# A perceiver block on one core: scores, values and side work of four attention steps in another order

## The chip, the cores and the metric

The kernel runs on one core of one Trainium2 chip. The time is the device time of one execution in microseconds: 961.16 us, the median of 3 runs (959.98 to 962.28). The profile shows another execution, which took 961.61 us.

## The reference, cut to what matters

```python
x = x + xattn(layernorm(x), ctx, ctx)   # x: 4 x 256 x 256, ctx: 4 x 4096 x 256, 16 heads of 16
x = x + attn(layernorm(x))              # linear attention by exponential features
x = x + ffn(layernorm(x))               # silu-gated, hidden size 768

# xattn:
Q, K, V = q @ Wq.T + bq, ctx @ Wk.T + bk, ctx @ Wv.T + bv
out = softmax(Q K^T / 4) V              # per head, 256 queries x 4096 keys
return out @ Wh.T + bh
# attn: per head causal, with features exp(clip(proj(x / |x|) * sqrt(2s) - s)) of q and k
```

All data are float32; some products run on high and low parts in a reduced float format.

## The kernel before, in words

There are four batches. The context of a batch, 4096 keys, is worked through in 8 chunks of 512 keys (`NCH`). A chunk has 16 steps (`STEPS`): a step takes 128 keys and 4 heads. Four steps are a quad, so a chunk has 4 quads, a batch 32 quads (128 steps), the kernel 128 quads.

A step has three parts. `fast_scores` (line 768, matmuls at L745) lets TensorE write the scores of 128 keys x 4 heads x 256 queries into one of two PSUM tiles ps_s, so it waits until the exponential of the step two before has read the tile. ScalarE takes the exponential into one of five buffers probs (L1011, `AHEAD`). `fast_values` (matmuls at L733) multiplies probs with the values and adds up in ps_o; it waits for its own exponential.

Between them lies side work, hung to step numbers: the slots. `fast_slot` of a step issues, on TensorE (line 782) and in the same order on VectorE (line 1347):
- projections of later chunks, into the one bank ps_p: values of the next chunk in steps 3 and 5 of a chunk (`VALUE_SLOTS`, L585), keys of the chunk after that in steps 9 and 13 (`KEY_SLOTS`, L552). VectorE copies them out (L1065; L1048 and L1050). In step 15 it also splits a piece of context into high and low parts (L1034, L1036);
- the stages of the tail of the batch before (everything behind the cross attention) and of the head of the next one (layernorm, queries, a bound for the scores), at the steps of the tables `AT` and `HEAD_AT` (counted within a batch). Nearly all of them write the one bank ps_a, which VectorE must have emptied before the next stage may write it. Stages named below: o, oT0, oT1 (1, 3, 4), ln1T, qk0, qk1 (24 to 26), qkT0, qkT1 (35, 36), feat0 to feat7 (feature products, L671, which VectorE clamps at L1249 and ScalarE exponentiates at L989), A0 to A15 (L677, L678), pv0 to pv3 (L682), y2T (91), wout (92, L615), ln2T (96, L607), gu0 to gu5 (gate products, L690, read by ScalarE, then by VectorE at L1259), down (121); of the head ln0T (102), q (106), max0 to max3 (112, 114, 116, 118).

The place of a slot is its step modulo 4. In the order before, a quad is: scores of places 0 and 1, their slots, scores of places 2 and 3, their slots, and then four value steps, which lag by two steps (`LAG`). In the first quad of a chunk the two value steps still due come between the halves and two come at the end. The first batch has no tail, the last no head.

ScalarE runs the exponentials in order of steps and takes the features and gates in between, where `ACT_BEHIND` says: behind the odd step of a pair.

Of the kernel before, what the change touches and what calls it, by code (L numbers as in the profile page):

```python
# [13 lines left out]
B, S, D = 4, 256, 256  # L14
# [13 lines left out]
QUAD = 2 * 2  # L28
# [19 lines left out]
LAG = 2  # L48
# [29 lines left out]
AT = {"o": 1, "oT0": 3, "oT1": 4, "yT": 19, "wh": 20, "ln1T": 24, "qk0": 25, "ss0": 25, "qk1": 26, "ss1": 26, "v": 28,  # L78
      "norm0": 34, "qkT0": 35, "norm1": 36, "qkT1": 36, "feat0": 37, **dict(zip(LINEAR, LINEAR_AT)),
      "o2T0": 88, "o2T1": 89, "y2T": 91, "wout": 92, "ln2T": 96, "gu0": 99, "gate0": 100, "gu1": 101, "gate1": 104,  # L80
      "gu2": 105, "gate2": 108, "gu3": 109, "gate3": 113, "gu4": 115, "gate4": 116, "gu5": 117, "gate5": 120,
      "down": 121}
# [5 lines left out]
FEATS = [f"feat{p}" for p in range(H // 2)]  # L88
GATES = [f"gu{k}" for k in range(HB)]

ACT_BEHIND = {**{n: 1 - AT[n] % 2 for n in FEATS}, **{n: 1 - AT[n] % 2 for n in GATES}}

NEEDS = {"maxT": "max3", "oT0": "o", "oT1": "o", "qk1": "ln1T", "v": "ln1T", "qkT0": "norm0", "qkT1": "norm1",
         **{n: "qkT1" for n in FEATS}, **{f"A{h}": "qkT1" for h in range(H)},
# [89 lines left out]
BS = NCH * STEPS  # L184
# [11 lines left out]
def perceiver(nc, x, ctxT, wqT, bq, wkT, bk, wvT, bv, whT, bh, wqkv, bqkv, wout, bout,  # L196
              omega, nodes, weights, wgT, wuT, wdT, out):
    ctx = ExitStack()
    with ctx:
# [120 lines left out]
        def tail_of(b):  # L320
            return (b + 2, b, True)

        def stages_at(b, step):

            return [(n, tail_of(of) if n in TAIL else head_of(of)) for of, n in stages_of(b, step)]
# [215 lines left out]
        def _(pe):  # L541
# [22 lines left out]
            def project_keys(q, j):  # L564

                pe.wait_ge(fast["ctx_split"], q + 1)
                if j:
                    pe.wait_ge(fast["k_out"], q * 2 + 1)
                elif q:
                    pe.wait_ge(fast["v_ready"], q * PAIRS)  # L570
                for part in range(CI):
                    project(fast, ("k", j, part), q, q % 2)

            def project_values(q, pair):

                if pair:
                    pe.wait_ge(fast["v_ready"], q * PAIRS + pair)
                else:
                    pe.wait_ge(fast["k_out"], q * 2 + 2)
                hi, lo = ctx_hi[q % 2], ctx_lo[q % 2]  # L580
                for t in range(2):
                    rows = slice((2 * pair + t) * P, (2 * pair + t + 1) * P)
                    for k in range(CI):
                        for n, (a, w) in enumerate(((hi, wv[0]), (lo, wv[0]), (hi, wv[1]))):
                            last = mm(ps_p[:, t * D:(t + 1) * D], a[:, k, rows], w[:, k, :],  # L585
                                      start=(t == 0 and k == 0 and n == 0), stop=(k == CI - 1 and n == 2),
                                      skip_group_check=True)
                last.then_inc(fast["v_proj"], 1)
# [123 lines left out]
            def products(c, names, clock, alone=False):  # L712
                for name in names:
                    if alone and c is fast:
                        warm(ps_o, WARM.get(name, 0))
                    if alone and name[:4] == "gate" and name != "gate0":

                        down_part(c, int(name[4:]) - 1, ps_a, clock)
                    if name not in VECTOR_ONLY:
                        stage(c, name, clock, alone)  # L720

            def value_product(c, n, s, par, starts, stops, vtile):

                i, g = s // G, s % G
                pe.wait_ge(c["exp_done"], n + (3 if c is general else 1))
                if c is general and g == 0:
                    pe.wait_ge(c["v_ready"], vtile + 2)
                elif c is fast and s % (STEPS // PAIRS) == 0:
                    pe.wait_ge(c["v_ready"], vtile // 2 + 1)
                prob = probs[s % NPROB if c is general else n % AHEAD]  # L730
                for j in range(GH):

                    last = mm(ps_o[32 * j:32 * j + DH + 1, g * S:(g + 1) * S],  # L733
                              values[par][:, i, head_of_step(g, j), :], prob[:, j * S:(j + 1) * S],
                              start=bool(starts and i == 0 and g % 2 == 0),
                              stop=bool(stops and i == TT - 1), skip_group_check=True)
                last.then_inc(c["pv_done"], 1)
# [30 lines left out]
            def fast_scores(b, q, s):  # L768

                n = q * STEPS + s  # L770
                if n >= LAG:
                    pe.wait_ge(fast["exp_done"], n - LAG + 1)
                score(fast, s, q % 2, qstacks[b % 2])

            def fast_values(n):

                b, q, s = n // BS, n // STEPS, n % STEPS
                if b and n % BS == 0:
                    pe.wait_ge(fast["operand"], fast.at("operand", tail_of(b - 1), "o"))
                value_product(fast, n, s, q % 2, q % NCH == 0, q % NCH == NCH - 1, q * TT + s // G)  # L780

            def fast_slot(b, p, s):

                q = b * NCH + p
                if s in VALUE_SLOTS and q + 1 < B * NCH:
                    project_values(q + 1, VALUE_SLOTS[s])
                if s in KEY_SLOTS and q + 2 < B * NCH:
                    project_keys(q + 2, KEY_SLOTS[s])
                for name, clock in stages_at(b, p * STEPS + s):
                    products(fast, [name], clock)  # L790
# [21 lines left out]
            for b in range(B):  # L812
                for p in range(NCH):
                    q = b * NCH + p
                    if p == 0:
                        pe.wait_ge(fast["q_stacked"], (b + 1) * Q_STACKED)
                        pe.wait_ge(fast["q_shift"], (b + 1) * 16)
                    if p == 0 and b == 1:
                        pe.wait_ge(late_in, 16 * 15)
                        pe.wait_ge(w_ready, 1)  # L820
                    if q < 2:
                        pe.wait_ge(hot_in, 16 * (q + 1))
                    pe.wait_ge(fast["k_stacked"][p % 2], (q // 2 + 1) * STACKED)
                    for s in range(0, STEPS, QUAD):
                        n = q * STEPS + s
                        for t in (0, 1):
                            fast_scores(b, q, s + t)
                        for t in (0, 1):
                            fast_slot(b, p, s + t)
                        if s == 0 and n:  # L830
                            for t in (0, 1):
                                fast_values(n - LAG + t)
                        for t in (2, 3):
                            fast_scores(b, q, s + t)
                        for t in (2, 3):
                            fast_slot(b, p, s + t)
                        for t in range(LAG if s == 0 else 0, QUAD):
                            fast_values(n - LAG + t)
            for t in range(LAG):
                fast_values(B * BS + t - LAG)  # L840
            products(fast, TAIL[:NORMALISED], tail_of(B - 1), True)

            pe.wait_ge(judged, 1)
# [133 lines left out]
        def _(act):  # L977
# [6 lines left out]
            def stage(c, name, clock, alone=False):  # L984
                if name in FEATS:
                    p = FEATS.index(name)

                    act.wait_ge(c["operand"], c.at("operand", clock, name))
                    nc.scalar.activation(feat[:, p % 2, :, :], feat[:, p % 2, :, :], ACT.Exp, bias=node_neg[:, :]  # L989
                                         ).then_inc(c["acted"], 1)  # L990
                else:
                    k = GATES.index(name)
                    act.wait_ge(c["product"], c.at("product", clock, name))
                    bank = bank_of(c, name, clock, alone)
                    nc.scalar.activation(gate_e[:, k % 2, :], bank[:, 0:S], ACT.Tanh, scale=QUANT / 2)
                    nc.scalar.activation(up[:, k % 2, :], bank[:, S:2 * S], ACT.Copy).then_inc(c["acted"], 1)
# [10 lines left out]
            for n in range(B * BS):  # L1007
# [5 lines left out]
                for name in FEATS + GATES:  # L1013
                    if n >= BS and AT[name] + ACT_BEHIND[name] == n % BS:
                        stage(fast, name, tail_of(n // BS - 1))
# [437 lines left out]
```

## Time and profile before

| | |
|---|---|
| median of 3 runs | 961.16 us (959.98 to 962.28) |
| the profiled execution | 961.61 us, span 959.9 us |
| TensorE busy | 872.1 us, 91% |
| TensorE weight loads | 608.0 us, 63% |
| ScalarE busy | 536.0 us, 56% |
| VectorE busy | 443.8 us, 46% |
| mean granted TensorE clock | 0.99 |
| chain that ended last | TensorE 73%, VectorE 11%, issue 6%, ScalarE 5% |

The attention steps run from 42.8 to 858 us; ahead of them lies the setup, behind them the tail of the last batch alone. Matmuls are pipelined: their durations overlap, so the time that a group takes is best read from its start to the start of the next. A clock of 1.00 is 2.4 GHz, 0.50 is 1.2 GHz.

### The profile page before, as it was taken

The numbers are of one execution on the slowest core, as the hardware profiler recorded it, in microseconds if no ns is written. First come the engines' busy times: TensorE is split into PE (matmuls) and PEld (weight loads), VectorE is DVE, ScalarE is ACT, GpSimd is POOL, SyncE is SP. The second block draws the span as 40 slices with busy tenths as digits, with TensorE's granted clock in tenths as the row PEclk, the third lists the DMA queues.
The fourth block names the chain that finished last, engine by engine and source line by source line (L and its number), as shares of the span: only waits on it lengthen the run. The fifth ranks groups of instructions, "written<-read, shape, count | busy, mean of one in ns | idle before, by whom it ended". The sixth has DMA issues, their size and how long they took to land.

```text
span 959.9 us, 20721 instructions
## 1 busy us (share of the span) xinstructions
PE 872.1 (91%) x8803; PEld 608.0 (63%) x8803; DVE 443.8 (46%) x847; ACT 536.0 (56%) x594; POOL 68.3 (7%) x124
## 2 busy tenths in 40 slices
PE   6799999999999988999999998999999999978676
PEld 5566666666566666666666665676666666656565
DVE  5522334554744345544743445535554444224553
ACT  2177777676565655656566555657566566840111
POOL 1033000000010000000011000000000000000120
PEclk9899999999999999999999999999999999999899
DMA  5666553566232333436233332345333331201000
GB/s 164 239 216 227 206 181 139 188 219 188 78 147 85 111 114 130 152 107 210 72 144 121 111 133 100 126 139 175 123 131 113 132 111 45 67 24 23 1 1 13
DMA packets 58736, 120.08 MB, mean 125 GB/s; under 512 B 21520, under 2 KB 29712, under 8 KB 55120
## 3 DMA queue, kind: packets, MB, share of 16 engines
q1 hardware_dynamic: 56848, 114.31, 34.6%
q0 software_dynamic: 1792, 4.40, 1.5%
q8 instruction: 71, 1.16, 0.5%
q14 instruction: 25, 0.20, 0.1%
HBM read 78.84 MB, written 37.75 MB: 121 GB/s over the span
## 4 chain that ended last, share of the span: by engine, by line
PE 73%; DVE 11%; issue 6%; ACT 5%; DVEq 2%; DMA 1%; POOL 1%; SPq 0%; ACTq 0%; POOLq 0%
PE ps_o L733 20%; PE ps_s L745 14%; PE ps_p L552 10%; PE ps_p L585 10%; ACT probs L1011 5%; PE ps_a L677 3%; PE ps_a L703 2%; PE ps_a L615 2%; PE ps_a L671 2%; PE ps_a L690 2%; DVE kparts L1050 1%; DVE kparts L1048 1%; PE ps_a L678 1%; DVE feat L1249 1%; PE ps_a L631 1%
## 5 line engine op out<-in xcount | busy, mean ns | idle before, releaser
L1011 ACT ACTIVATE probs<-ps_s 128x1024 f32<-128x1024 f32 x512 | 495.5, 1025 | 263.8 <-PE ps_s L745 236.1
L733 PE MATMUL ps_o<-probs,values 128*17 128x256 f32 x4096 | 252.0, 381 | 0.0
L745 PE MATMUL ps_s<-qstack,kstack 64*128 64x256 f32 x2048 | 201.4, 309 | 19.3 <-ACT probs L1011 18.5
L745 PEld LDWEIGHTS ps_s<-qstack,kstack 64*128 64x128 f32 x2048 | 140.7, 185 | 121.1 <-ACT probs L1011 65.1
L733 PEld LDWEIGHTS ps_o<-probs,values 128*17 128x17 f32 x4096 | 105.2, 97 | 93.1 <-issue 7.3
L1048 DVE TENSOR_SCALAR kparts<-ps_p,b_heads 128x512 fp32r<-128x512 f32 x64 | 48.0, 750 | 114.1 <-PE ps_p L552 114.0
L1065 DVE TENSOR_TENSOR values<-ps_p,bv_pair 128x512 f32<-128x512 f32 x64 | 44.2, 691 | 88.5 <-PE ps_p L585 88.5
L989 ACT ACTIVATE feat<-feat,node_neg 128x512 f32<-128x512 f32 x32 | 23.1, 722 | 105.4 <-DVE feat L1249 105.4
L585 PE MATMUL ps_p<-wv_hi,ctx_hi 128*128 128x256 f32 x256 | 78.6, 307 | 1.6 <-DVE wv_lo L1036 1.6
L585 PE MATMUL ps_p<-wv_hi,ctx_lo 128*128 128x256 f32 x256 | 72.3, 283 | 0.0
L585 PE MATMUL ps_p<-wv_lo,ctx_hi 128*128 128x256 f32 x256 | 72.3, 282 | 0.0
L552 PE MATMUL ps_p<-ctx_hi,wk_hi 128*128 128x512 f32 x128 | 58.8, 459 | 4.0 <-DVE ctx_lo L1036 2.2
L1253 DVE TENSOR_TENSOR amat<-ps_a,causal 128x384 f32<-128x384 f32 x48 | 26.7, 556 | 77.2 <-PE ps_a L678 77.2
L948 POOL TENSOR_TENSOR kfeat<-feat,half_mask 128x256 f32<-128x256 f32 x64 | 37.8, 612 | 313.7 <-ACT feat L989 313.7
L585 PEld LDWEIGHTS ps_p<-wv_hi,ctx_hi 128*128 128x128 f32 x256 | 48.4, 189 | 5.9 <-DVE wv_lo L1036 1.8
L552 PE MATMUL ps_p<-ctx_lo,wk_hi 128*128 128x512 f32 x128 | 51.9, 406 | 0.0
L552 PE MATMUL ps_p<-ctx_hi,wk_lo 128*128 128x512 f32 x128 | 51.7, 404 | 0.0
L1050 DVE SCALAR_TENSOR_TENSOR kparts<-ps_p,b_heads,kparts 128x512 fp32r<-128x512 f32 x64 | 48.1, 751 | 4.9
L585 PEld LDWEIGHTS ps_p<-wv_hi,ctx_lo 128*128 128x128 f32 x256 | 48.5, 190 | 0.5
L585 PEld LDWEIGHTS ps_p<-wv_lo,ctx_hi 128*128 128x128 f32 x256 | 48.5, 189 | 0.0
L1036 DVE TENSOR_TENSOR ctx_lo<-ctx_raw,ctx_hi 128x1024 fp32r<-128x1024 f32 x32 | 39.2, 1226 | 2.4
L914 POOL TENSOR_TENSOR rstd<-veps,half_power 128x2 f32<-128x2 f32 x12 | 8.3, 690 | 429.7 <-DVE veps L1078 429.7
(213 smaller groups left out, 892.5 us busy)
## 6 DMA issues: line engine op xcount, KB each, us to landing
kstack<-kscr SPq DMA_DIRECT2D x96, 512.0 KB, 5.0
kscr<-kparts SPq DMA_DIRECT2D x64, 512.0 KB, 2.7
ctx_raw<-ctxT SPq DMA_DIRECT2D x32, 512.0 KB, 6.7
qstack<-qscr SPq DMA_DIRECT2D x12, 256.0 KB, 3.6
qscr<-qparts SPq DMA_DIRECT2D x4, 512.0 KB, 2.9
xh<-x SPq DMA_DIRECT2D x4, 256.0 KB, 6.9
kstack<-kstack SPq DMA_DIRECT2D x2, 512.0 KB, 6.5
qstack<-ksample SPq DMA_DIRECT2D x4, 256.0 KB, 3.7
```

The lines of the kernel that those rows point to most:

```text
L552: last = mm(ps_p[:, :], w[:, k, j * P:(j + 1) * P], a[:, k, :], start=(k == 0 and n == 0), stop=(k == CI - 1 and n == 2))
L585: last = mm(ps_p[:, t * D:(t + 1) * D], a[:, k, rows], w[:, k, :], start=(t == 0 and k == 0 and n == 0), stop=(k == CI - 1 and n == 2), sk ...
L677: mm(bank[:, 0:S], kfeat[:, p % 2, n % 2, 0:P], feat[:, p % 2, 0, :], start=True, stop=True)
L733: last = mm(ps_o[32 * j:32 * j + DH + 1, g * S:(g + 1) * S], values[par][:, i, head_of_step(g, j), :], prob[:, j * S:(j + 1) * S], start=b ...
L745: last = mm(ps_s[s % 2][:, j * S:(j + 1) * S], kstack[par][rows, u, i * P:(i + 1) * P], queries[rows, u, :], start=True, stop=True)
L948: pool.tensor_tensor(kfeat[:, p % 2, k, :], feat[:, p % 2, 1, :], half_mask[:, k:k + 1].to_broadcast([P, S]), ALU.mult).then_inc(c["kfeat" ...
L1011: nc.scalar.activation(probs[n % AHEAD][:, :], ps_s[n % 2][:, :], ACT.Exp, scale=float(DH) ** -0.5).then_inc(fast["exp_done"], 1)
L1036: return v.tensor_tensor(lo, src, hi.bitcast(FP32), ALU.subtract)
L1048: v.tensor_scalar(kparts[:, 0, j, :], ps_p[:, :], bias, None, ALU.add)
L1050: v.scalar_tensor_tensor(kparts[:, 1, j, :], ps_p[:, :], bias, kparts[:, 0, j, :].bitcast(FP32), ALU.add, ALU.subtract).then_inc(c["k_out" ...
L1065: v.tensor_tensor(values[q % 2][:, 2 * pair:2 * pair + 2, :, 0:DH].rearrange("p t h d -> p (t h) d"), ps_p[:, :].rearrange("p (n d) -> p n ...
L1253: last = v.tensor_tensor(amat[:, n % GH, :], bank[:, 0:3 * P], causal[:, :], ALU.mult)
```

## The change

The quad gets another order on TensorE: scores of places 0 and 1, four value steps (those of the quad before), scores of places 2 and 3, then the slots of all four places. The values now lag by four steps, at the start of a chunk too; the four that are left come at the end. ScalarE takes features and gates behind the last step of the quad. VectorE's order, GpSimd's and SyncE's stay.

```diff
-ACT_BEHIND = {**{n: 1 - AT[n] % 2 for n in FEATS}, **{n: 1 - AT[n] % 2 for n in GATES}}
+ACT_BEHIND = {n: QUAD - 1 - AT[n] % QUAD for n in FEATS + GATES}
...
                         for t in (0, 1):
                             fast_scores(b, q, s + t)
-                        for t in (0, 1):
-                            fast_slot(b, p, s + t)
-                        if s == 0 and n:
-                            for t in (0, 1):
-                                fast_values(n - LAG + t)
+                        if n:
+                            for t in range(QUAD):
+                                fast_values(n - QUAD + t)
                         for t in (2, 3):
                             fast_scores(b, q, s + t)
-                        for t in (2, 3):
+                        for t in range(QUAD):
                             fast_slot(b, p, s + t)
-                        for t in range(LAG if s == 0 else 0, QUAD):
-                            fast_values(n - LAG + t)
-            for t in range(LAG):
-                fast_values(B * BS + t - LAG)
+            for t in range(QUAD):
+                fast_values(B * BS + t - QUAD)
```

TensorE in batch 1, from the last key projection and feat2 in the last quad of a chunk to the first quad of the next chunk, before (x8 at L745 are two score steps, x16 at L733 four value steps, which the trace counts as x32):

```order
L552 MATMUL ps_p<-ctx_lo,wk_hi 128x512
L671 MATMUL ps_a<-qkT,om_sb 128x256 x2
L745 MATMUL ps_s<-qstack,kstack 128x256 x8
L677 MATMUL ps_a<-feat,kfeat 128x256
L678 MATMUL ps_a<-feat,kfeat 128x128
L733 MATMUL ps_o<-probs,values 17x256 x16
L745 MATMUL ps_s<-qstack,kstack 128x256 x8
L733 MATMUL ps_o<-probs,values 17x256 x8
L745 MATMUL ps_s<-qstack,kstack 128x256 x8
L677 MATMUL ps_a<-feat,kfeat 128x256
L678 MATMUL ps_a<-feat,kfeat 128x128
```

The same piece now:

```order
L552 MATMUL ps_p<-ctx_lo,wk_hi 128x512
L671 MATMUL ps_a<-qkT,om_sb 128x256 x2
L677 MATMUL ps_a<-feat,kfeat 128x256
L678 MATMUL ps_a<-feat,kfeat 128x128
L745 MATMUL ps_s<-qstack,kstack 128x256 x8
L733 MATMUL ps_o<-probs,values 17x256 x16
L745 MATMUL ps_s<-qstack,kstack 128x256 x8
L677 MATMUL ps_a<-feat,kfeat 128x256
L678 MATMUL ps_a<-feat,kfeat 128x128
```

The two score steps between the feature product L671 and the next product of ps_a, L677, are gone from there; at the chunk's start four value steps stand between the score pairs instead of two.

TensorE in batch 1 around ln2T (L607), in the first quad of chunk 6, before; behind the last row come the rest of the value projection and then gu0 at L690:

```order
L552 MATMUL ps_p<-ctx_lo,wk_hi 128x512
L745 MATMUL ps_s<-qstack,kstack 128x256 x8
L733 MATMUL ps_o<-probs,values 17x256 x16
L745 MATMUL ps_s<-qstack,kstack 128x256 x8
L607 MATMUL ps_a<-ident,xn 128x128 x4
L733 MATMUL ps_o<-probs,values 17x256 x8
L745 MATMUL ps_s<-qstack,kstack 128x256 x8
L585 MATMUL ps_p<-wv_hi,ctx_hi 128x256
```

And now:

```order
L552 MATMUL ps_p<-ctx_lo,wk_hi 128x512
L745 MATMUL ps_s<-qstack,kstack 128x256 x8
L733 MATMUL ps_o<-probs,values 17x256 x16
L745 MATMUL ps_s<-qstack,kstack 128x256 x8
L607 MATMUL ps_a<-ident,xn 128x128 x4
L585 MATMUL ps_p<-wv_hi,ctx_hi 128x256
```

Two value steps and two score steps no longer stand between ln2T and the value projection.

## Rows read from the trace of the kernel before

**Rows 1.** The page: its head and the busy time of TensorE

```profile
span 959.9 us, 20721 instructions
PE 872.1 (91%) x8803; PEld 608.0 (63%) x8803; DVE 443.8 (46%) x847; ACT 536.0 (56%) x594; POOL 68.3 (7%) x124
```

**Rows 2.** Waits of TensorE: engine, line, waited for: us in total, times, longest

```profile
PE ps_s L745 <- ACT probs L1011: 18.5, 44, 0.9
...
PE ps_s L666 <- DVE qk L1243: 5.3, 1, 5.3
...
PE ps_a L844 <- DVEq L1367: 2.7, 1, 2.7
```

**Rows 3.** Timeline, a chunk's start in batch 0: start, us, engine, line, operation, count, idle

```profile
60.96 1.92 PE L733 MATMUL ps_o<-probs,values 128*17 128x256 f32 x32
...
62.81 0.74 PE L745 MATMUL ps_s<-qstack,kstack 64*128 64x256 f32 x8
63.36 3.77 ACT L1011 ACTIVATE probs<-ps_s 128x1024 f32<-128x1024 f32 x4 [0.62 <-PE ps_s L745]
63.48 1.06 PE L733 MATMUL ps_o<-probs,values 128*17 128x256 f32 x16
64.47 0.50 PE L745 MATMUL ps_s<-qstack,kstack 64*128 64x256 f32 x4
65.35 0.50 PE L745 MATMUL ps_s<-qstack,kstack 64*128 64x256 f32 x4 [0.38 <-ACT probs L1011]
65.78 0.39 PE L585 MATMUL ps_p<-wv_hi,ctx_hi 128*128 128x256 f32 x1
```

**Rows 4.** Timeline of TensorE, scores behind feature feat4 in batch 1

```profile
304.46 0.50 PE L745 MATMUL ps_s<-qstack,kstack 64*128 64x256 f32 x4 [0.67 <-ACT probs L1011]
```

**Rows 5.** Timeline of TensorE, batch 1: around feat2, y2T, ln0T

```profile
278.93 1.02 PE L671 MATMUL ps_a<-qkT,om_sb 128*128 128x256 f32 x4
279.88 0.74 PE L745 MATMUL ps_s<-qstack,kstack 64*128 64x256 f32 x8
281.48 0.70 PE L677 MATMUL ps_a<-feat,kfeat 128*128 128x256 f32 x2 [0.85 <-DVE feat L1249]
...
359.79 0.66 PE L607 MATMUL ps_a<-ident,y 128*128 128x128 f32 x4 [1.48 <-DVE y L1115]
...
383.01 0.66 PE L607 MATMUL ps_a<-ident,xh 128*128 128x128 f32 x4 [0.61 <-DVE amat L1259]
```

**Rows 6.** Timeline, batch 1: qk0, norm0 on VectorE, qkT0

```profile
243.22 1.88 PE L660 MATMUL ps_a<-wqkv_sb,xT 128*128 128x512 f32 x4
...
259.87 0.69 DVE L1243 TENSOR_TENSOR qk<-qk,rnorm 128x512 f32<-128x512 f32 x1
...
261.29 0.60 PE L666 MATMUL ps_a<-ident,qk 128*128 128x128 f32 x4
```

**Rows 7.** Timeline of TensorE, batch 1: first matmul behind wout, first of gu0

```profile
364.54 0.58 PE L552 MATMUL ps_p<-ctx_hi,wk_hi 128*128 128x512 f32 x1
...
376.31 0.39 PE L690 MATMUL ps_a<-x_hi,wg 128*128 128x256 f32 x1 [2.93 <-DVE x_lo L1036]
```

**Rows 8.** Timeline, batch 0: max0, its reduction on VectorE, max1

```profile
186.27 0.50 PE L637 MATMUL ps_a<-ksample,qparts 128*128 128x512 f32 x1
...
187.94 0.68 DVE L1175 TENSOR_REDUCE neg_max<-ps_a 128x8 f32<-128x512 f32 x1
...
188.68 0.50 PE L637 MATMUL ps_a<-ksample,qparts 128*128 128x512 f32 x1
```

**Rows 9.** Stretches: busy time of each engine, granted clock, DMA share, GB/s

```profile
373.50:376.20 2.70, 0.00 (x0) 0.00 (x0) 2.55 (x5) 0.00 (x0) 0.00 (x0) 1.00 0.84 309
890.50:892.90 2.40, 0.00 (x0) 0.00 (x0) 2.00 (x6) 0.00 (x0) 0.00 (x0) 0.50 0.00 0
893.00:896.90 3.90, 3.90 (x19) 3.90 (x20) 1.38 (x2) 0.00 (x0) 0.00 (x0) 0.50 0.01 2
...
863.30:866.20 2.90, 2.90 (x14) 2.90 (x15) 0.42 (x2) 0.00 (x0) 0.00 (x0) 0.50 0.66 78
```

## The prediction

> **What bounds the kernel now.** I read the page first. The span is 959.9 us and TensorE is busy for 91% of it [rows 1]; the profiled execution took 961.61 us and the median of the runs shown is 961.16 us. So what counts is the time in which TensorE, between about 43 and 858 us, has nothing to do. The list of waits names the first sort: 44 score groups wait 18.5 us for exponentials [rows 2]. The second sort is TensorE waiting for VectorE (or for ScalarE and then VectorE) to empty the single bank ps_a. I then read the timeline of TensorE quad by quad, always from the start of a group to the start of the next, since the durations overlap.
>
> Three prices come from one stretch of batch 0 [rows 3]: a pair of score steps behind value steps takes 62.81 to 63.48 = 0.67 us; four value steps 60.96 to 62.81 = 1.85; two value steps 63.48 to 64.47 = 0.99. The exponentials start 0.55 after the first score group (62.81 to 63.36) and take 3.77 / 4 = 0.94 each. A score step needs the buffer of the step two before, so S2 cannot start before 0.55 + 0.94 + about 0.17 = 1.66 after S0; it started at 64.47, exactly that. S3 follows 0.88 later, idle 0.38.
>
> **What goes away.** At a chunk's first quad the slots of places 0 and 1 are mostly empty, and two value steps don't fill the time of an exponential. Before, such a quad costs 0.67 + 0.99 + (65.78 - 64.47 = 1.31) + slots + 0.99 = 3.96 + slots [rows 3]. Now: 0.67 + 1.85 + 0.67 = 3.19 + slots. S2 would start 2.52 after S0 (needed 1.66), S3 at 2.86 (needed 2.6): both covered. Saved 0.77. I count 21 such quads: chunks 1 to 6 of batch 0, and chunks 0, 1, 3, 4, 5 of the three others; chunks 2, 6, 7 of those have terms of their own below. 21 x 0.77 = -16.2. In the last quad of all nothing but scores and values is left, and there the score waits are longest, 0.9 [rows 2]; the four value steps now cover them, but two more value steps are left for the end. I take -1.1 (an estimate), and -0.6 for the gate quads just before it, whose short score waits move but get fewer. Together **-17.9**.
>
> The score waits behind feature products stay. At 304.46 the scores wait 0.67 because ScalarE stood at the feature's exponential until VectorE had clamped it [rows 4]. Before, a feature in place 0 or 1 is followed by score pair, four values, next score pair, which waits. Now it is followed by next score pair, four values, score pair: the same 2.52 of cover, so the same wait, one quad on. Priced at nothing; were the queue behind it worse, it would be one exponential, 0.94, at four features in each of three batches, +11; were it hidden, at most 12 x 0.67 = -8.
>
> **What is added.** First, slots that lay on both sides of S2 and S3 are now neighbours. At 278.93 a feature product, at 279.88 the score pair, at 281.48 the next product of ps_a after 0.85 idle for VectorE's clamp [rows 5]. The distance 279.88 to 281.48 = 1.60 is set by VectorE alone, whose key work comes first. The 0.67 of scores that lay in it now lie elsewhere, so the quad gets 0.67 longer. The same holds at y2T (idle 1.48 [rows 5]) and where a gate product is followed by ln0T (idle 0.61 [rows 5]), q or max3: in each, the pair did not fill the gap. Places: three feature quads and y2T in batches 1 to 3 (12), three gate quads in batches 1 and 2 (6): 18 x 0.67 = **+12.1**. The Trainium skill (Perfetto Trace Analysis, Optimizing Tensor Performance, Matmuls) wants independent matmul groups to rotate through PSUM banks so that evacuation overlaps the next group. It speaks against this change: ps_a does not rotate, and the score pair was the only other-bank work there. With rotation this term would be 0; the trace, with its idle, goes by the rule.
>
> Second, chains on VectorE that begin in place 0 or 1 start later in their quad: S0 S1 no longer precede them alone but S0 S1, V x 4, S2 S3, which is 2.52 later, while their reader in place 3 of a chunk's first quad is hardly moved.
> - qk0 to qkT0. qk0 starts at 243.22; VectorE then works without a pause up to norm0, 259.87 + 0.69 = 260.56; qkT0 was ready at 261.29 [rows 6]. 2.52 later the chain ends at 263.1, qkT0 ends at 263.7; before, this quad ended with its two values at 261.82 + 0.99 = 262.8. So the three quads together lose 0.9, x 3 batches = **+2.7**, which includes the saving of that chunk's start.
> - wout to gu0. wout ends at 364.54, gu0 starts at 376.31, 11.77 later, after 2.93 idle: VectorE does layernorm, keys, the next batch's layernorm, a context split and x_lo in a row [rows 7]. Now wout ends 2.52 later in its quad and the 11.77 remain. Before, from there: 11.77 + 1.14 (gu0) + 0.98 (values) = 13.89; now 2.52 + 11.77 + 1.14 = 15.43: 1.54 in batches 1 and 2 (in batch 3 VectorE has no next batch to serve) = **+3.1**.
> - max0 to max1. The reduction of max0 ran 187.94 to 188.62 and max1 started at 188.68, 2.41 after max0 at 186.27 [rows 8]. Two values and a score pair lay between. Now nothing does, and max1 must still wait: 0.67 + 1.85 + 0.67 + 2.41 + 1.84 (max1, projection) = 7.44 against 0.67 + 2.41 + 1.84 + 0.99 = 5.91: +1.5, a little less in batches 1 and 2, together **+4.3**.
>
> Sum so far: 22.2 - 17.9 = +4.3.
>
> **The clock.** In the wout quad TensorE goes idle once ln2T and the value projection are done, about 1.66 + 3.19 + 0.58 + 1.7 = 7.1 after wout's end, and gu0 comes at 11.77: 4.6 us with nothing to do, twice. Rows on both sides [rows 9]: through most of the 2.93 us idle before 376.31 the granted clock stayed at 1.00 (2.4 GHz); in the 5.3 us idle of L666 [rows 2], which ends at 893, it fell to 0.50 (1.2 GHz) and was still 0.50 at 896.9, 3.9 us after work came back; after the 2.7 us idle of L844 [rows 2], which ends at 863.3 and has only a microsecond of work ahead of it, it was 0.50 for 2.9 us of work. 4.6 is nearer to 5.3 than to 2.93, and longer than one of the two that lost the clock. At half the clock 2.9 to 3.9 us of matmuls lose 1.5 to 2.0; I take 1.75 x 2 = **+3.5** (bounds 0 and 4). The Trainium skill (TensorE: Matmul & The Clock Gate, Part 1: The HAM clock gate) calls the reduced clock the default that activity releases; by that rule an idle stretch costs twice, and rows 9 agree in two of three stretches.
>
> Sum: +4.3 + 3.5 = +7.8 on 961.61 = 969.4; against the median 961.16, 969.0. VectorE's small waits before oT1 and qkT1, which get more cover, may give back up to 1. I forecast **968.5 us**. Instructions are only reordered; DMAs are the same, and SyncE's waits see scores and operands at nearly the same times. Probs have five buffers: exp(n+1) needs value step n-4, the first behind S1, done at 0.67 + 0.46 while exp(n) runs until 1.49: free, thinly.
>
> **Rivals.**
> 1. *The clock stays* up through 4.6 us, as it did through 2.93. For: rows 9's first stretch. Against: the two others. 965.0.
> 2. *Other side: the neighbours do not wait.* If the pieces in ps_a's gaps were paid by VectorE finishing sooner once less is queued ahead of it, the +12.1 and the chains would shrink. The place is the 1.60 at 279.88, the price 0.67 per place; below 17.9 of the 22.2 it decides for faster, and with none of them the time is 961.2 - 17.9 = 943. Against: VectorE's order is unchanged, and the gap starts at the projection's end in both.
> 3. *ScalarE late everywhere.* S3 has 0.3 us of cover. If something delays the exponentials by 0.5 us in each ordinary quad, some 100 quads lose 0.25: +25, 994. Against: in quads with a projection (1.6 us) ScalarE's 3.77 fits 4.8.
> 4. *It cancels*: the clock stays and VectorE has more slack than I read at the chains, so that their 2.7 + 3.1 + 4.3 is halved: 4.3 - 5 = -0.7, 960.5. For: max0 and qk1 had other work queued ahead of them that I did not trace. Against: rows 6 to 8 show VectorE ending just before its reader starts.
>
> **Chances.** Forecast 0.68 (966 to 972); rival 1 0.14; rival 2 0.06; rival 3 0.05; rival 4 0.07. About 0.2% (1.9 us) is what a measurement of this kernel tells from no change: rival 2 is faster, 0.06; rival 4 and a little of rival 1 are the same, 0.09; the rest slower, 0.85. The range 963.5 to 972 leaves out rivals 2, 3 and 4, some 0.18.
>
> **What would show it.** Score waits on probs should drop from 44 to about 20, and none of 0.38 be left at chunk starts; batch 0 should be some 4 us shorter up to its last quad, a chunk there 19.3 us instead of 20.05. L677 after L671, the second L607 and L631 should wait about 1.4 us each; L690 should wait some 4.6 us twice, with the clock at 0.50 behind it. Wrong it would be if ps_a waits stay at their old lengths, if L690 waits 3 us, or if batches 1 and 2 get shorter.

## The result and the profile after

| | kernel before | changed kernel |
|---|---|---|
| median of 4 runs each, us | 960.57 (959.50 to 962.28) | 975.79 (974.75 to 976.29) |
| ratio, 95% interval | | 1.0155 [1.0137, 1.0174] |
| profiled execution, its span, us | 961.61, 959.9 | 974.75, 973.0 |
| granted clock of the profiled execution | 0.990 | 0.973 |

The forecast was 968.5 with a range of 963.5 to 972. The sign is right, the time is outside the range: the change costs 15.2 us where some 8 were forecast. Between the two profiled executions it is 13.1 us of span; the missing 2.1 is which executions were profiled (before's lies 1.04 above its median, the changed kernel's 1.04 below).

The page of the changed kernel, its head and the busy time; TensorE has as much work as in [rows 1], in a longer span:

```profile
span 973.0 us, 20721 instructions
PE 871.2 (90%) x8803; PEld 613.3 (63%) x8803; DVE 443.8 (46%) x847; ACT 537.2 (55%) x594; POOL 68.2 (7%) x124
```

The waits of TensorE in the changed kernel (engine, tile and line, what is waited for: us in total, times, longest). Lines behind the edit have moved up by four: L1007 was L1011, L1245 was L1249, L1171 was L1175.

```profile
PE ps_a L677 <- DVE feat L1245: 9.1, 6, 1.5
PE ps_a L690 <- DVE x_lo L1032: 9.1, 2, 4.5
PE ps_a L637 <- DVE neg_max L1171: 8.5, 5, 2.6
PE ps_s L745 <- ACT probs L1007: 7.9, 18, 0.9
PE ps_a L607 <- DVE y L1111: 6.4, 3, 2.1
...
PE ps_a L682 <- DVE amat L1249: 4.4, 3, 1.5
...
PE ps_a L666 <- DVE qk L1239: 3.0, 3, 1.0
...
PE ps_s L745 <- issue: 1.6, 2, 1.1
```

Against [rows 2] the score waits fell from 44 (18.5 us) to 18 (7.9), where about 20 were forecast. Nearly all that rose waits for VectorE, which must first empty the bank ps_a (feat, neg_max, amat) or write what TensorE reads next (x_lo, y, qk): before, the same list gave feat 5.1, x_lo 5.8, neg_max 3.5, y 4.4, amat of L682 2.4, and no wait of L666 on ps_a. The last row, score waits for nothing that the profile names, was 0.5.

A chunk's start of batch 0 (timeline: start, length, engine, line, operation, count, idle before it), to be held against [rows 3]:

```profile
61.56 0.78 PE L745 MATMUL ps_s<-qstack,kstack 64*128 64x256 f32 x8
...
62.27 1.92 PE L733 MATMUL ps_o<-probs,values 128*17 128x256 f32 x32
64.12 0.74 PE L745 MATMUL ps_s<-qstack,kstack 64*128 64x256 f32 x8
...
64.79 0.39 PE L585 MATMUL ps_p<-wv_hi,ctx_hi 128*128 128x256 f32 x1
```

No score group waits; the quad is over 3.2 after its start. The same projection comes at 64.79 now and 65.78 before, and at 161.22 against 166.01 five chunks on: 0.76 won a chunk, where 0.77 was forecast.

### The profile page after: what moved, and what is told of

It is laid out like the page before. It is cut to its first block, busy times and chain, and to the rows that moved or that the text cites. A ratio compares the mean times of both kernels' runs of the same rounds, so it can differ in the third digit from the quotient of the medians.

```text
span 973.0 us, 20721 instructions
## 1 busy us (share of the span) xinstructions
PE 871.2 (90%) x8803; PEld 613.3 (63%) x8803; DVE 443.8 (46%) x847; ACT 537.2 (55%) x594; POOL 68.2 (7%) x124
## 4 chain that ended last, share of the span: by engine, by line
PE 73%; DVE 14%; issue 5%; ACT 3%; DVEq 2%; DMA 1%; POOL 1%; SPq 0%; POOLq 0%; ACTq 0%
PE ps_o L733 21%; PE ps_s L745 15%; PE ps_p L552 9%; PE ps_p L585 9%; PE ps_a L677 3%; PE ps_a L703 2%; ACT probs L1007 2%; PE ps_a L671 2%; DVE kparts L1046 2%; PE ps_a L690 2%; DVE kparts L1044 2%; DVE ctx_lo L1032 1%; PE ps_a L615 1%; PE ps_a L678 1%; DVE feat L1245 1%
## 5 line engine op out<-in xcount | busy, mean ns | idle before, releaser
L1007 ACT ACTIVATE probs<-ps_s 128x1024 f32<-128x1024 f32 x512 | 496.0, 1023 | 265.4 <-PE ps_s L745 263.8
L733 PE MATMUL ps_o<-probs,values 128*17 128x256 f32 x4096 | 248.7, 384 | 0.3 <-ACT probs L1007 0.3
L745 PE MATMUL ps_s<-qstack,kstack 64*128 64x256 f32 x2048 | 195.5, 308 | 9.8 <-ACT probs L1007 7.9
L745 PEld LDWEIGHTS ps_s<-qstack,kstack 64*128 64x128 f32 x2048 | 140.1, 186 | 97.7 <-ACT probs L1007 61.4
L733 PEld LDWEIGHTS ps_o<-probs,values 128*17 128x17 f32 x4096 | 107.4, 98 | 95.8 <-issue 3.7
L1249 DVE TENSOR_TENSOR amat<-ps_a,causal 128x384 f32<-128x384 f32 x48 | 26.7, 556 | 76.6 <-PE ps_a L678 76.6
L677 PE MATMUL ps_a<-feat,kfeat 128*128 128x256 f32 x96 | 31.7, 412 | 9.1 <-DVE feat L1245 9.1
```

The source lines that it names most:

```text
L677: mm(bank[:, 0:S], kfeat[:, p % 2, n % 2, 0:P], feat[:, p % 2, 0, :], start=True, stop=True)
L733: last = mm(ps_o[32 * j:32 * j + DH + 1, g * S:(g + 1) * S], values[par][:, i, head_of_step(g, j), :], prob[:, j * S:(j + 1) * S], start=b ...
L745: last = mm(ps_s[s % 2][:, j * S:(j + 1) * S], kstack[par][rows, u, i * P:(i + 1) * P], queries[rows, u, :], start=True, stop=True)
L1007: nc.scalar.activation(probs[n % AHEAD][:, :], ps_s[n % 2][:, :], ACT.Exp, scale=float(DH) ** -0.5).then_inc(fast["exp_done"], 1)
L1249: last = v.tensor_tensor(amat[:, n % GH, :], bank[:, 0:3 * P], causal[:, :], ALU.mult)
```

## Where the time went

Batch 1 in the changed kernel, timeline of TensorE: feat2 and what follows it, y2T, then from wout's end to gu0:

```profile
277.35 1.02 PE L671 MATMUL ps_a<-qkT,om_sb 128*128 128x256 f32 x4
279.90 0.70 PE L677 MATMUL ps_a<-feat,kfeat 128*128 128x256 f32 x2 [1.52 <-DVE feat L1245]
...
358.19 1.11 PE L607 MATMUL ps_a<-ident,y 128*128 128x128 f32 x4 [2.14 <-DVE y L1111]
359.23 1.22 PE L745 MATMUL ps_s<-qstack,kstack 64*128 64x256 f32 x8
...
365.03 0.58 PE L552 MATMUL ps_p<-ctx_hi,wk_hi 128*128 128x512 f32 x1
...
369.88 0.66 PE L607 MATMUL ps_a<-ident,xn 128*128 128x128 f32 x4
376.79 0.58 PE L690 MATMUL ps_a<-x_hi,wg 128*128 128x256 f32 x1 [4.53 <-DVE x_lo L1032]
...
378.80 1.22 PE L745 MATMUL ps_s<-qstack,kstack 64*128 64x256 f32 x8
```

From feat2 to the next product are 2.55, before 0.95 + 1.60 = 2.55 [rows 5]: the distance stayed and the score pair fell out of it. From wout's end to gu0 are 11.76, before 11.77 [rows 7]: VectorE's chain is what it was, and TensorE now stands idle for 4.53 of it. But look at the lengths: the transposes of y2T take 1.11 where they took 0.66 [rows 5], a score pair 1.22 instead of 0.74. The stretches (busy time of PE, PEld, DVE, ACT, POOL with counts, granted clock, DMA share, GB/s) say why, the last three in the tail:

```profile
358.00:361.40 3.40, 3.21 (x24) 2.13 (x28) 1.42 (x3) 1.02 (x1) 0.00 (x0) 0.50 0.40 154
...
375.00:378.50 3.50, 1.71 (x8) 1.71 (x8) 2.26 (x4) 0.00 (x0) 0.00 (x0) 0.51 0.96 300
378.50:381.90 3.40, 3.40 (x30) 1.84 (x33) 0.85 (x2) 2.45 (x4) 0.00 (x0) 0.50 0.62 241
...
607.00:610.50 3.50, 3.50 (x33) 1.79 (x35) 0.84 (x2) 2.63 (x4) 0.00 (x0) 0.50 0.58 229
...
873.40:880.30 6.90, 5.74 (x28) 5.74 (x29) 1.32 (x7) 0.00 (x0) 0.00 (x0) 0.51 0.38 45
...
890.40:894.00 3.60, 3.60 (x5) 1.52 (x6) 0.00 (x0) 0.00 (x0) 0.00 (x0) 0.53 0.00 0
...
904.00:911.00 7.00, 4.86 (x23) 4.87 (x24) 3.21 (x7) 0.00 (x0) 0.00 (x0) 0.51 0.00 1
```

The clock is at 1.2 GHz behind the idle of 2.14 us at y2T of batch 1 and for some 5 us of work behind each of the two idles of 4.53 and 4.54. Between the attention's start and the tail the kernel before has no such stretch. By the lengths of the groups (gu0 2.01 instead of 1.14, score pair 1.15 instead of 0.67, value steps 2.78 instead of 1.85, the last partly) this costs 1.4 at y2T and 2.3 and 2.4 at the two gu0. In batches 2 and 3 y2T waits just as long and takes 0.66, at a granted clock of 1.00:

```profile
588.02 0.66 PE L607 MATMUL ps_a<-ident,y 128*128 128x128 f32 x4 [2.14 <-DVE y L1111]
...
816.49 0.66 PE L607 MATMUL ps_a<-ident,y 128*128 128x128 f32 x4 [2.14 <-DVE y L1111]
```

The tail begins with L647, before and in the changed kernel:

```profile
859.45 1.09 PE L647 MATMUL ps_s<-ident,qk 128*128 128x128 f32 x8 [1.35 <-DVE qk L1213]
```

```profile
870.75 1.09 PE L647 MATMUL ps_s<-ident,qk 128*128 128x128 f32 x8 [1.35 <-DVE qk L1209]
```

So it comes 11.3 later, and the tail alone went from 100.45 to 102.25 us, with about 17 instead of about 10 us at half the clock: 1.8 more. That the clock is the whole of these 1.8 is read from the stretches; no run changed the tail by itself.

What no step had: a transfer. The queue of SyncE in the changed kernel, and the scores of batch 1 that need what it brings:

```profile
199.68 0.37 SPq L369 DMA_DIRECT2D kscr<-kparts  x1
200.09 0.66 SPq L415 DMA_DIRECT2D qstack<-ksample  x1
...
203.93 0.74 PE L745 MATMUL ps_s<-qstack,kstack 64*128 64x256 f32 x8 [1.10 <-issue]
```

The shift rows of the next batch's queries are issued behind a key write that waits for its projection. The transfer takes 3.84 from issue to scores (200.09 to 203.93). Before, it was issued at 201.92 for scores that started at 207.13, 1.4 more than it needs. Now TensorE is there at 202.83, 4.3 sooner, and the issue comes only 1.8 sooner, so the scores wait 1.10.

The chains are priced by the distance between the same two projections in both traces: across max0 and max1 from 11.06 to 12.61, 12.83 to 14.10 and 12.85 to 14.13 (batches 0 to 2); across wout and gu0 from 29.54 to 35.44 and 29.53 to 34.17 (batches 1 and 2), of which 0.67 each is y2T's neighbour and 3.7 and 2.4 the clock. The three quads of qk0 to qkT0 took 22.14, 22.15 and 22.13 and now take 23.05, 22.72 and 22.72.

| term | forecast | measured |
|---|---|---|
| chunk starts, last and gate quads | -17.9 | -17.5 as what is left; 0.76 a chunk was read at five places of batch 0 |
| neighbours, 18 places | +12.1 | +11.9 (feat +4.0, amat +2.0, y +2.0, and +1.3 each at L607, L631, L637) |
| qk0 to qkT0 | +2.7 | +0.91, +0.57, +0.59 |
| wout to gu0 | +3.1 | +1.5, +1.6 without the clock; 11.76 as before, idle 4.53 and 4.54 |
| max0 to max1 | +4.3 | +1.55, +1.27, +1.28; distance 185.52 - 183.11 = 2.41, as in [rows 8] |
| clock | +3.5 | +7.9 = 1.4 + 2.3 + 2.4 + 1.8 |
| shift transfer, a value projection | none | +1.1, +0.4 |
| sum | +7.8 | 3.7 + 7.9 + 1.5 = 13.1, the difference of the spans |

The 3.7 for everything that the order does by itself is 11.3 up to the tail, less 6.1 of clock and the 1.5 of the transfer and the projection. It was forecast at 4.3; the miss lies in the clock and in what was not priced.

## Experiments

Times are compared with the kernel before on the same chip, whose own median was 963 to 965 on these chips (959.3 to 969.5 in single runs, at granted clocks of 0.991 to 0.977, the longer ones mostly at the lower).

**The changed kernel again.** No edit.

> The changed kernel once more, unchanged, beside the kernel before on the chip that the next three run on. If the change costs the same on every chip, the ratio is 1.0155 again (1.0137 to 1.0174 so far), about 15 us above the kernel before. The rival: part of the 15 us belongs to the chip or to where the clock happened to fall, and the ratio comes out nearer to the predicted 1.008.

Measured: 975.35 (973.48 to 976.33), ratio 1.0105 [1.0069, 1.0141]. The changed kernel takes the same time on another chip to half a microsecond; the kernel before takes 2.7 more. So of the 15.2 some 12 to 15 are the change's, depending on the chip, and the forecast 8 is below both. Neither expectation was quite met.

**Filling the idles.** Dummy matmuls, a first time too many:

```diff
+FILL = {"y2T": 17, "gu0": 38}
...
+                    count = FILL.get(name, 0) if b < B - 1 or name == "y2T" else 0
+                    if count:
+                        pe.wait_ge(fast["exp_done"], q * STEPS + s + 1)
+                        warm(ps_s[1], count)
```

> The changed kernel with dummy 128x128 matmuls into the free score buffer ps_s[1] while TensorE waits: 17 ahead of y2T (3 places) and 38 ahead of gu0 (batches 1 and 2); they add nothing to the output. Theory A (the clock): the waits of 2.1 us (y2T) and 4.5 us (gu0) let the granted clock fall to 0.50, and the matmuls behind them lost 1.4, 2.3 and 2.4 us in the profiled execution; with the clock kept at 1.00 the time falls by 4 to 6 us, from 975.8 to about 970.5, and gu0 takes 1.1 us instead of 2.0. Rival B (only the waits count, the clock is incidental): 975.8, within 1 us. If the fillers are too long for the gaps: slower by up to 1 us.

Measured: 982.74, ratio 1.0172 [1.0140, 1.0204]; a miss. The clock did stay at 1.00 behind gu0, but 38 calls are 76 matmuls in the trace and took 8.64 us where 4.5 were idle. Half the count:

```diff
+FILL = {"y2T": 8, "gu0": 19}
```

> The changed kernel with 8 short dummy matmuls before y2T and 19 before gu0, each behind the exponentials of its quad, so that TensorE is busy through these idles and hardly longer than they are (a call measured 0.22 us, so 1.8 us against the idle of 2.1 and 4.2 against 4.5). Clock theory: the falls behind y2T of batch 1 (+1.4), gu0 of batch 1 (+2.3) and gu0 of batch 2 (+2.4) are gone, so some 6 us under the changed kernel on the same chip, granted clock 1.00 at gu0. Rival (the clock falls for another reason, at these places whatever TensorE does): no faster than the changed kernel, granted clock still 0.50 behind gu0.

Measured: 968.30, ratio 1.0037 [1.0010, 1.0064], 7.05 under the changed kernel on the same chip. Its timeline and stretches at gu0 of batch 1:

```profile
372.01 4.40 PE L711 MATMUL ps_s<-ident 128*128 128x128 f32 x38
376.69 0.39 PE L691 MATMUL ps_a<-x_hi,wg 128*128 128x256 f32 x1 [0.27 <-DVE x_lo L1037]
```

```profile
372.00:376.40 4.40, 4.40 (x40) 4.22 (x38) 3.62 (x6) 0.00 (x0) 0.59 (x1) 1.00 0.62 222
377.00:382.00 5.00, 5.00 (x64) 3.58 (x63) 1.08 (x3) 3.59 (x6) 0.00 (x0) 1.00 0.66 226
```

gu0 starts when it did (376.69, 376.79), nothing useful was added, and the work behind runs at 2.4 GHz. So the clock behind these idles is worth about 7 by the medians, 6.1 by the three places read above. The forecast had 3.5 for it. The 1.8 of the tail are not in this measurement: its trace shows the same three slow stretches there.

**Shorter idle instead of filled.** `HEAD_AT = {"ln0": 98,` in place of 94: VectorE does the next batch's layernorm behind x_lo.

> The changed kernel with one table entry changed: the next batch's layernorm ln0 at step 98 instead of 94, so that VectorE does ln2T's split first. Theory (VectorE's chain from wout to gu0 is what TensorE waits for, and the idle stretch is paid twice through the clock): the chain of 11.77 us gets shorter by ln0's 2.9 us, gu0 waits 1.6 instead of 4.5 us, the clock stays: -5.8 - 4.7 = about -10, to 965.5. Without the double payment: -5.8, 970. If another resource ends the wait (the value projection, the context split alone): 975.8, no change.

Measured: 969.37, ratio 1.0042 [1.0018, 1.0066]: 6 under the changed kernel where 9 to 10 were expected. By the time alone it would be the case "without the double payment", 970; the trace shows that the wait did what was said and the clock did not:

```profile
PE ps_a L690 <- DVE x_lo L1032: 3.1, 2, 1.6
```

```profile
358.00:361.50 3.50, 3.38 (x24) 2.08 (x28) 1.35 (x3) 1.07 (x2) 0.00 (x0) 0.53 0.41 154
375.50:379.00 3.50, 3.50 (x38) 1.49 (x36) 2.09 (x5) 2.25 (x4) 0.52 (x1) 0.55 0.92 347
```

It still falls behind y2T of batch 1, and in batch 1 even with an idle of 1.56 ahead of gu0: gu0 itself runs at full clock, the scores and values behind it do not.

**The transfer.** The shift queries issued ahead of the key write instead of behind it:

```diff
+                    if b + 1 < B and p == HEAD_AT["maxT"] // STEPS:
+                        shift_queries(fast, head_of(b + 1), qstacks[(b + 1) % 2])
...
-                    if b + 1 < B and p == HEAD_AT["maxT"] // STEPS:
-                        shift_queries(fast, head_of(b + 1), qstacks[(b + 1) % 2])
```

> The changed kernel with SyncE's queue in another order at a batch's end: the shift of the queries (behind maxT) is issued ahead of the key write of step 121 instead of behind it. Theory: the 1.1 us for which the first scores of batch 1 wait, with nothing named in the list of waits, is this transfer, issued too late: -1.1, to 974.7. Rival: it is another wait (keys stacked, weights ready): 975.8. Batches 2 and 3 have 5 us of down products in between and should not change.

Measured: 975.24, ratio 1.0104 [1.0075, 1.0134]. In its trace the transfer is issued at 197.98 and batch 1 starts at 203.26 without an idle of 1.10, though its attention began 0.55 later than the changed kernel's. So the wait is gone in the trace. The time is within 0.6 of the expected one, but a gain of 1.1 is less than times can tell here.

**Where ScalarE takes the features.** The old places in its order under TensorE's new one:

```diff
-ACT_BEHIND = {n: QUAD - 1 - AT[n] % QUAD for n in FEATS + GATES}
+ACT_BEHIND = {**{n: 1 - AT[n] % 2 for n in FEATS}, **{n: 1 - AT[n] % 2 for n in GATES}}
```

> The changed kernel with the features and gates back at the places in ScalarE's order that they had before (behind the exponential of their own pair of steps), TensorE's order as changed. Theory: in the changed order a feature product of slots 0 and 1 stands behind the second score pair, so ScalarE stands at the feature while the exponentials of steps 2 and 3 are ready; the next scores wait for them: 12 features and gates in slots 0 and 1 by some 1 to 2 us each and batch, slower than the changed kernel by 20 to 60 us. Rival (ScalarE's place does not matter): within 3 us of the changed kernel.

Measured: 1061.54, ratio 1.0999 [1.0955, 1.1043], 86 above the changed kernel. Its timeline in batch 1:

```profile
306.04 0.72 ACT L985 ACTIVATE feat<-feat,node_neg 128x512 f32<-128x512 f32 x1 [5.42 <-DVE feat L1245]
306.67 2.83 ACT L1007 ACTIVATE probs<-ps_s 128x1024 f32<-128x1024 f32 x3
...
307.73 0.50 PE L745 MATMUL ps_s<-qstack,kstack 64*128 64x256 f32 x4 [3.19 <-ACT probs L1007]
```

ScalarE stands 5.42 us at the feature while exponentials are ready, and the scores wait 3.19. The mechanism is the expected one, larger than expected. Idle before L745 rose from 9.8 to 56.7 us, so 47 of the 86 are score waits; the rest is not separated, the lower clock (0.946 against 0.973) is part of it. So the edit of ScalarE's places is a needed half of the change and not a part of the loss.

**Where the value steps must stand.** Three orders that keep the lag of four and put side stages back between the score pairs. First, all slots in their pairs and the value steps behind the first:

```diff
                         for t in (0, 1):
                             fast_scores(b, q, s + t)
+                        for t in (0, 1):
+                            fast_slot(b, p, s + t)
                         if n:
                             for t in range(QUAD):
                                 fast_values(n - QUAD + t)
...
-                        for t in range(QUAD):
+                        for t in (2, 3):
                             fast_slot(b, p, s + t)
```

> Four value steps between the score pairs as in the changed kernel, but the slots stay split: scores 0 1, slots 0 1, four values, scores 2 3, slots 2 3. Theory (the loss comes from slots that became neighbours, and from VectorE's chains starting 2.52 us later in their quad): both go, the chunk starts keep their 0.77 each, and the waits on ps_a that the kernel before had (feature, y2T, gate stages, about 20 us) are covered by 2.5 us of values and scores as well: 961 - 18 - 20 = 920 to 925. Rival (the loss comes from the lag of four or from where ScalarE takes features and gates): this kernel is as slow as the changed one, 970 or more. In between, if only the chunk starts gain: 943.

Measured: 1100.40, ratio 1.1405; the theory failed. Waits of its TensorE and ScalarE:

```profile
PE ps_s L745 <- ACT probs L1009: 100.6, 167, 1.0
```

```profile
ACT probs L1009 <- PE ps_o L733: 293.3, 120, 8.9
```

exp(n+1) needs the buffer of value step n-4, which now stood behind the slots. That is the thin cover the prediction named. In the changed kernel, whose value steps stand directly behind S1, ScalarE's waits for L733 are 1.4 us in 3.

Second, the value steps behind S1 again, side stages of slots 0 and 1 behind them, all projections behind S3 (lines of the new order, set against the changed kernel; the value steps stood there before too, and the last two slots follow):

```diff
+                        for t in range(QUAD) if n else ():
+                            fast_values(n - QUAD + t)
+                        for t in (0, 1):
+                            fast_slot(b, p, s + t)
                         for t in (2, 3):
                             fast_scores(b, q, s + t)
+                        fast_projection(q, s + 1)
```

> The changed kernel with the side stages of the first two slots of a quad put back between the four value steps and the second pair of scores (projections stay behind the second pair; ScalarE's and VectorE's orders follow). Keeps the lag of four and the value steps between the score pairs at every chunk start. Theory (the loss is side stages in neighbouring slots that now stand back to back on one bank): the waits of y, feat, neg_max, qk and x_lo go back to the kernel before or under it, 22 us of waits and 6 to 8 us of clock less than the changed kernel: about 20 us under it, 5 to 15 us UNDER the kernel before, since the 17.9 us saved at the chunk starts stay. Rival (the lag of four and ScalarE's position cost by themselves): not faster than the kernel before, with score waits on ScalarE above 20 us in sum.

Measured: 1008.32, ratio 1.0432 [1.0383, 1.0481]; a second miss. Two of its waits:

```profile
PE ps_a L671 <- DVE amat L1256: 5.9, 9, 0.7
...
PE ps_a L677 <- DVE amat L1256: 3.9, 6, 0.7
```

Without the projection of slot 1 between them, slots 0 and 1 had become neighbours themselves; and two side stages plus a score pair ahead of S2 left ScalarE's exponentials late (score waits 13.4 us in 29). The 33 us are not accounted for in full.

Third, side stages spread so that a projection, or two value steps and a score pair, stands between any two:

```diff
+                        for t in (0, 1) if n else ():
+                            fast_values(n - QUAD + t)
+                        fast_slot(b, p, s)
+                        for t in (2, 3) if n else ():
+                            fast_values(n - QUAD + t)
                         for t in (2, 3):
                             fast_scores(b, q, s + t)
-                        for t in range(QUAD):
+                        for t in (1, 2, 3):
                             fast_slot(b, p, s + t)
```

and in slot 1 the side stage ahead of the projection, on TensorE and VectorE.

> The changed kernel with the side stages spread over the quad: two score steps, two value steps, the side stage of slot 0, two value steps, two score steps, then slots 1 to 3, and in slot 1 the side stage ahead of the projection (on VectorE too), so that a projection (1.6 us) or value and score steps (1.6 us) stand between any two side stages. Lag of four and ScalarE's places as in the changed kernel. Theory (the loss is side stages back to back on one bank, and the clock that falls behind their idles): y, feat, neg_max, qk and xn/qkT waits together under 12 us against some 37, no half clock before the tail; with the 17.9 us of the chunk starts kept: about 950, between 943 and 957, under the kernel before by 6 to 20. Rival (any interposed work delays the next scores' exponentials as in the run where value steps came behind the slots): score waits above 30 us and the time at or above the changed kernel's 975.

Measured: 955.02 (952.05 to 959.60), ratio 0.9909 [0.9883, 0.9935]: 20 under the changed kernel (975.35, on another chip) and 8 under the kernel before. Score waits are 2.2 us in 6, and of the waits for the next stage's bank or operand those of feat, y and L666 on ps_a are gone from the list; the largest left between the attention's start and the tail are these:

```profile
PE ps_a L615 <- DVE qk L1230: 7.8, 3, 2.6
PE ps_s L745 <- issue: 5.5, 4, 1.8
...
PE ps_a L690 <- DVE x_lo L1041: 5.2, 2, 2.6
PE ps_a L637 <- DVE ksample L1175: 4.4, 3, 1.6
```

The expected clock was wrong again: 0.50 came back at six places of batches 1 to 3, as here at gu0 of batch 2.

```profile
591.50:595.00 3.50, 3.32 (x20) 2.86 (x24) 1.14 (x3) 1.14 (x3) 0.00 (x0) 0.50 0.94 296
```

With the two small edits from above (ln0 at 98, shift queries first):

> The run before it, with ln0's place moved from step 94 to 98 and the transfer of the shift queries issued ahead of the key halves. Theory: the wait before gu0 falls by some 3 us in two batches and the 1.1 us wait of batch 1's first scores is gone: 4 to 7 us under the run before it, about 945. Rival (both are covered once the stages are apart): within 1 us of it.

Measured: **941.48** (940.98 to 944.73), ratio 0.9778 [0.9735, 0.9821], the fastest of all. It gains 13.5 over the run before it, where 4 to 7 were expected: the waits for x_lo are gone (5.2) and those for the transfer nearly (5.5 to 0.5), and with fewer idles there is less time at half the clock (about 10 us of it in batches 1 to 3 in its trace, against about 24). The trace of the run before it is of its slowest execution, 959.60 where the median is 955.02, so it shows more slow clock than most.

**Controls on these two edits.** With TensorE's order as changed, plus 8 dummy matmuls ahead of y2T:

> TensorE's order as changed; ln0 at step 98, the shift queries ahead of the key halves, and 8 dummy matmuls before y2T. Theory: of the changed kernel's 975 it saves the 3 us of idle twice, the clock behind gu0 (4.7) and behind y2T (1.4) and the 1.1 us transfer: about 963, level with the kernel before, since the neighbours' 22 us still eat the 17.9 of the chunk starts. Rival (the clock falls elsewhere instead): 968 or more.

Measured: 966.28 (959.11 to 967.98), ratio 1.0020 [0.9997, 1.0043], between the expected 963 and the rival's 968. On the kernel before:

> The kernel before with the same two edits that went on top of the spread order (ln0 at step 98, the shift queries issued ahead of the key halves). Theory: the order is what makes the fastest run fast; here the edits can take back only the wait before gu0 (5.8 us in two) by some 3 to 5 us and no transfer, so 958 to 961 where the kernel before shows 963. Rival (the two edits, not the order, make the gain): 945 or less.

Measured: 956.70, ratio 0.9929 [0.9906, 0.9953]. So the small edits give 7 us in the old order, where 2 to 5 were expected, and the spread order, against 941.48, the other 15. Of the 7 the wait for x_lo ahead of gu0 (5.8 before) is gone in the trace. But that trace also begins its attention steps at 39.92, where the kernel before began at 42.77, and neither edit acts ahead of that; how much of the 7 comes from such a start is open.

## Why the prediction was off

- *Which waits go* held: 18 score waits left, 0.76 a chunk start in batch 0, which is shorter by 4.1 from its first scores up to its last quad (42.77 to 202.31 before, 42.57 to 197.97 now).
- *The neighbours and the three chains* held, place by place: distances of 2.55, 11.76 and 2.41 that VectorE sets, with the score pair fallen out of them; only qk0 to qkT0 cost less than said in batches 2 and 3. With the chunk starts they make 3.7 where the prediction had 4.3. The run with the stages spread shows the cause: with 1.6 us of other work between them the same lag of four is faster than the kernel before. It moves more than one thing (slot 1's order too), so it confirms the sum of the neighbours, not each.
- *The clock* is the step that failed, in size and in its bounds: 7.9 where 3.5 was forecast and 4 was the most. It took 1.75 per idle of 4.6 and nothing elsewhere. Each gu0 cost 2.3 to 2.4, since the work behind stayed at 1.2 GHz for some 5 us; one of the three idles of 2.14 at y2T cost 1.4; and the tail, in which nothing was reordered, 1.8. The filled idles gave back 7.05. The step listed [rows 9]'s 2.7 us case behind which the clock was down, and still asked only about the two idles of 4.6. The bound should have taken in every place where an idle grew, and the tail. Which of these places lose the clock in an execution no run here lets one say beforehand.
- "*SyncE's waits see scores and operands at nearly the same times*" failed: one transfer had 1.4 us to spare, TensorE came 4.3 us sooner and the issue 1.8, and 1.1 us was lost. It is small, but nothing in the sum had priced it. In the run with the stages spread the score waits for which the profile names nothing are 5.5 us.
- *Rival 1*, the clock stays: wrong, the stretches and the fills show it. *Rival 2*, the neighbours do not wait: wrong in the trace. *Rival 3*, ScalarE late everywhere: not in this kernel, but the order with the value steps behind the slots fell into it (167 waits, 100.6 us), so its cover is as thin as stated. *Rival 4*, it cancels: wrong; the chains were of the length read.

## What to carry over

When work that separates two users of one bank moves, the price is the length of that work per place, and it can be counted from the timeline: 18 x 0.67 came out as 11.9. Then look for an order in which other work takes the gap, before giving up the gain elsewhere: here that took the change from 12 to 15 us above the kernel before to 8 below. And when a change makes TensorE's idles longer, read off the row what the work behind them costs at the low clock, at every such place and in the tail, and take that as the term rather than as an extra.

## What the runs showed of the hardware

The granted clock does not follow the length of an idle alone: idles of 2.93 and 2.90 before gu0 kept it at 1.00 in the kernel before, and in one execution of the changed kernel three idles of 2.14 ahead of y2T ended once at 0.50 and twice at 1.00. With ln0 moved it fell even behind an idle of 1.56.

It also varies from one execution to the next: single runs of the kernel before took 959.3 to 969.5 us, with mean granted clocks between 0.991 and 0.977. Part of that can lie ahead of any work discussed here: over all the traces of this case the first scores of the attention come between 39.25 and 43.12 us, with the stretches at half clock in the setup at different places. So a difference of 2 or 3 us between two traces is to be read from the first scores on.

A dummy product of `warm` is two matmuls in the trace, and 19 of them took 4.40 us.
